# A language model's block on one core: fp16 halves transposed by DMA from SyncE instead of by TensorE

## The reference

```
h = rms_norm(rms_norm(emb[x]) @ proj.T)
h = h + attn(layernorm(h))        # 16 heads of 32; squared scores, causal, divided by their sum
                                  # ... o @ Wo.T
h = h + ffn(layernorm(h))         # fwht(x * SU_ug), gate and up (512 -> 2048), silu(gate) * up,
                                  # fwht(a * SU_dp), down (2048 -> 512)
```

## Time and profile before

| | |
|---|---|
| median of 3 runs | 1439.61 us (1438.97 to 1442.25) |
| the profiled execution | 1439.44 us, of which the span is 1437.6 us |
| granted TensorE clock, mean of the span | 0.97 of full speed |
| PE busy | 1331.6 us, 93% |

### The profile page before, as it was taken

One profiled execution on the slowest core, in us unless ns is written; L12 is line 12 of the kernel. 1 busy time (PEld: TensorE's weight loads), 2 busy tenths in 40 slices (PEclk: granted clock), 3 DMA queues, 4 the chain that ended last, 5 costly groups with the idle time before them and its releaser, 6 DMA issues.

```text
span 1437.6 us, 20304 instructions
## 1 busy us (share of the span) xinstructions
PE 1331.6 (93%) x7989; PEld 673.4 (47%) x7989; DVE 524.0 (36%) x1039; ACT 457.4 (32%) x767; POOL 418.1 (29%) x372
## 2 busy tenths in 40 slices
PE   5566439998999999999999999999999999999998
PEld 3455215554444544544444444444445445444444
DVE  1456695322522252224322442234322622251110
ACT  3475424432224312331234123322332224312220
POOL 0234212233134322442134214331343224420210
PEclk9889769999999999999999999999999999999999
DMA  9211000000100010001000010001000100010000
GB/s 332 93 61 67 22 8 1 1 1 22 38 8 1 8 45 16 1 1 47 21 0 1 30 38 1 1 23 38 8 0 9 44 16 1 1 45 15 1 1 30
DMA packets 21453, 39.41 MB, mean 27 GB/s; under 512 B 6212, under 2 KB 6520, under 8 KB 20856
## 3 DMA queue, kind: packets, MB, share of 16 engines
q1 hardware_dynamic: 17856, 28.99, 5.8%
q0 software_dynamic: 2560, 8.39, 2.0%
q10 hardware_dynamic: 952, 0.75, 0.2%
HBM read 29.47 MB, written 8.65 MB: 27 GB/s over the span
## 4 chain that ended last, share of the span: by engine, by line
PE 88%; DVE 6%; ACT 3%; issue 1%; DMA 1%; POOL 0%; SPq 0%; DVEq 0%; ACTq 0%
PE bank L1009 25%; PE bank L1010 25%; PE bank L1011 25%; PE bank L1153 3%; PE bank L1004 2%; PE bank L1138 2%; PE bank L1139 2%; ACT sg L778 2%; DMA wgu<-in_L_attn_Wv 1%; PE bank L1040 1%; PE bank L1173 1%; PE bank L1163 1%; PE bank L1002 1%; PE bank L1078 0%; DVE hid L410 0%
## 5 line engine op out<-in xcount | busy, mean ns | idle before, releaser
L1009 PE MATMUL bank<-xT,wgu 128*128 128x512 f16 x1024 | 389.1, 380 | 4.2 <-DVE xT L667 4.2
L1010 PE MATMUL bank<-xT,wgu 128*128 128x512 f16 x1024 | 389.1, 380 | 0.0
L1011 PE MATMUL bank<-xT,wgu 128*128 128x512 f16 x1024 | 389.1, 380 | 0.0
L365 POOL TENSOR_TENSOR hid<-a,hid 128x512 f16<-128x512 f32 x128 | 147.8, 1155 | 518.3 <-ACT hid L781 518.3
L701 DVE SCALAR_TENSOR_TENSOR a<-bank,kap,sg 128x512 f32<-128x512 f32 x128 | 96.1, 750 | 517.2 <-PE bank L1011 360.3
L1011 PE MATMUL bank<-wd,hid 128*128 128x512 f16 x512 | 194.8, 381 | 0.0
L1010 PE MATMUL bank<-wd,hid 128*128 128x512 f16 x512 | 194.8, 381 | 0.0
L1009 PE MATMUL bank<-wd,hid 128*128 128x512 f16 x512 | 194.8, 380 | 0.0
L337 POOL TENSOR_TENSOR p<-prod,p 128x512 f16<-128x512 f32 x128 | 149.0, 1166 | 133.8 <-ACT p L781 133.8
L781 ACT ACTIVATE hid<-a 128x512 f16<-128x512 f32 x128 | 80.6, 630 | 277.2 <-DVE a L701 277.2
L1011 PEld LDWEIGHTS bank<-xT,wgu 128*128 128x128 f16 x1024 | 100.3, 98 | 121.4 <-issue 1.1
(11 more groups left out here) (181 smaller groups left out, 1365.3 us busy)
## 6 DMA issues: line engine op xcount, KB each, us to landing
out<-a SPq DMA_DIRECT2D x24, 256.0 KB, 2.1
ids_b<-in_x SPq DMA_DIRECT2D x8, 256.0 KB, 4.0
hid<-in_L_ffn_W_gate SPq DMA_DIRECT2D x2, 1024.0 KB, 11.8
hid<-in_L_ffn_W_up SPq DMA_DIRECT2D x2, 1024.0 KB, 12.8
wd<-in_L_ffn_W_gate SPq DMA_DIRECT2D x2, 1024.0 KB, 11.7
wd<-in_L_ffn_W_up SPq DMA_DIRECT2D x2, 1024.0 KB, 10.1
hid<-in_L_ffn_W_down SPq DMA_DIRECT2D x2, 1024.0 KB, 4.8
wd<-in_L_ffn_W_down SPq DMA_DIRECT2D x2, 1024.0 KB, 4.8
```

Of the source, the lines that this page charges most:

```text
L365: nc.gpsimd.tensor_tensor(hid[:, 1, s, :], a32[:, :], hid[:, 0, s, :], ALU.subtract)\
L1009: mm(dst, w[0], v[0], start=first, stop=False)
L1010: mm(dst, w[0], v[1], start=False, stop=False)
L1011: return mm(dst, w[1], v[0], start=False, stop=final)
```

## The change

The 8 transposes on PE and the copy on ACT, for each q and each m, become one DMA transpose of the whole 128x1024 fp16 tile (256 KB), which SP issues: `o_turn(n, q)` from o16 to oT, and `x_turn(n, m)` from x16 to xn16. The slots O_FLIP_AT and X_FLIP_AT go. Waits move with them: ACT may overwrite x16 and o16 when the transfer has landed; the first gather of a block waits for the first Wo product (wo_ready) instead of the last transpose; and SP's loop over blocks is written out. SP's order while block b is fed becomes: o_turn 0 to 3, x_turn 0, store 0, x_turn 1, store 1, x_turn 2, ids_b, store 2, x_turn 3, ids_c, store 3. In the preparation the four loads of w_down and the eight turns of block 0 are mixed.

```diff
...
-O_FLIP_AT = (5, 9, 13, 17)
...
-X_FLIP_AT = (21, 23, 25, 27)
...
-        oT = sb("oT", [P, 2, QUADS, T], F16)
+        oT = sb("oT", [P, QUADS, 2, T], F16)
...
-            norm_load(2, 16)
-            norm_load(0, 20)
-            norm_load(1, 24)
...
+            def o_turn(n, q):
+                if n and q == 0:
+                    sp.wait_ge(S["wo_ready"], 4 * n)
+                sp.wait_ge(S["ol_done"], QUADS * n + q + 1)
+                nc.sync.dma_start_transpose(oT[:, q, :, :].rearrange("p l (m t) -> p (l m) t", t=P),
+                                            o16.rearrange("p l d -> p (l d)")).then_inc(S["oT_done"], 16)
+
+            def x_turn(n, m):
+                sp.wait_ge(S["xl_done"], 4 * n + m + 1)
+                if n or m:
+                    sp.wait_ge(S["xhada_ready"], 4 * n + m)
+                nc.sync.dma_start_transpose(xn16.rearrange("p (k t) -> p k t", t=P),
+                                            x16.rearrange("p l d -> p (l d)")).then_inc(S["xc_done"], 16)
+
+            def block_io(b, n, turning):
+
+                for q in range(QUADS):
+                    if turning is not None:
+                        o_turn(turning, q)
+                if turning is not None:
+                    x_turn(turning, 0)
                 for m in range(4):
                     if n is not None and m == 2:
                         load_ids_rows(n)
@@ -274,15 +287,24 @@
                         sp.wait_ge(S["y_done"], 3 * b + m + 1)
                     else:
                         sp.wait_ge(S["y_last_done"], b + 1)
-                    nc.sync.dma_start(out_rows[bass.ds(b, 1), m, :, :].rearrange("a p d -> (a p) d"), o_out[m][:, :])\
+                    nc.sync.dma_start(out_rows[b, m, :, :], o_out[m][:, :])\
                         .then_inc(S["stored"], 16)
+                    if turning is not None and m < 3:
+                        x_turn(turning, m + 1)
 
             load_ids_rows(1)
+            o_turn(0, 0)
+            norm_load(2, 16)
+            o_turn(0, 1)
+            norm_load(0, 20)
+            norm_load(1, 24)
+            o_turn(0, 2)
+            o_turn(0, 3)
+            for m in range(4):
+                x_turn(0, m)
             load_ids_columns(1)
-            with sp.Fori(0, NB - 2) as b:
-                block_io(b, b + 2)
-            block_io(NB - 2, None)
-            block_io(NB - 1, None)
+            for b in range(NB):
+                block_io(b, b + 2 if b + 2 < NB else None, b + 1 if b + 1 < NB else None)
...
-                    pool.wait_ge(S["o_flipped"], QUADS * n + QUADS)
+                    pool.wait_ge(S["wo_ready"], 4 * n + 1)
                     pool.wait_ge(S["h1_done"], 4 * n + m)
...
+                    if not (isinstance(n, int) and n == 0 and q == 0):
+                        act.wait_ge(S["oT_done"], 16 * (QUADS * n + q))
                     copy(o16[:, 0, :], wide[:, :]).then_inc(S["oh_done"], 1)
-                if s in O_FLIP_AT:
-                    q = O_FLIP_AT.index(s)
-                    act.wait_ge(S["o_flipped"], QUADS * n + q + 1)
-                    if q == 0:
-                        act.wait_ge(S["wo_ready"], 4 * n)
-                    copy(oT[:, :, q, :], banks[6][:, :].bitcast(F16).rearrange("p (l t) -> p l t", l=2))\
-                        .then_inc(S["oT_done"], 1)
-                if s in X_FLIP_AT:
-                    m = X_FLIP_AT.index(s)
-                    act.wait_ge(S["flip_ready"], 4 * n + m + 1)
-                    act.wait_ge(S["xhada_ready"], 4 * n + m)
-                    copy(xn16, PICK[0][:, :].bitcast(F16)).then_inc(S["xc_done"], 1)
                 if s in X_MIX_AT:
                     m = X_MIX_AT.index(s)
...
-                    act.wait_ge(S["flip_ready"], 4 * n + m)
+                    if not (isinstance(n, int) and n == 0 and m == 0):
+                        act.wait_ge(S["xc_done"], 16 * (4 * n + m))
                     copy(x16[:, 0, :], wide[:, :], scale=rstd[:, m:m + 1]).then_inc(S["xh_done"], 1)
...
-                    pe.wait_ge(S["oT_done"], QUADS * n + q)
+                    if not (isinstance(n, int) and n == 0 and q == 0):
+                        pe.wait_ge(S["o_done"], QUADS * n + q)
...
-                if s in O_FLIP_AT:
-                    q = O_FLIP_AT.index(s)
-                    pe.wait_ge(S["ol_done"], QUADS * n + q + 1)
-                    bank = banks[6][:, :].bitcast(F16)
-                    for l in range(2):
-                        for m in range(4):
-                            c = (4 * l + m) * P
-                            last = nc.tensor.transpose(bank[:, c:c + P], o16[:, l, m * P:(m + 1) * P], ident16)
-                    last.then_inc(S["o_flipped"], 1)
-                if s in X_FLIP_AT:
-                    m = X_FLIP_AT.index(s)
-                    pe.wait_ge(S["xl_done"], 4 * n + m + 1)
-                    pe.wait_ge(S["xc_done"], 4 * n + m)
-                    bank = PICK[0][:, :].bitcast(F16)
-                    for i in range(2):
-                        for k in range(DC):
-                            c = (DC * i + k) * P
-                            last = nc.tensor.transpose(bank[:, c:c + P], x16[:, i, k * P:(k + 1) * P], ident16)
-                    last.then_inc(S["flip_ready"], 1)
                 if s in X_MIX_AT:
                     m = X_MIX_AT.index(s)
-                    pe.wait_ge(S["xc_done"], 4 * n + m + 1)
+                    pe.wait_ge(S["xc_done"], 16 * (4 * n + m + 1))
                     pe.wait_ge(S["xT_done"], 4 * n + m)
...
-                        pe.wait_ge(S["oT_done"], QUADS * n + QUADS)
+                        pe.wait_ge(S["oT_done"], 16 * (QUADS * n + QUADS))
...
-                        last = split_mm(WOUT[m % 2][:, :], [oT[:, i, k, c] for i in range(2)],
+                        last = split_mm(WOUT[m % 2][:, :], [oT[:, k, i, c] for i in range(2)],
                                         [wo_t[:, i, k, :] for i in range(2)], k == 0, k == DC - 1)
...
```

More of the change, by code:

```diff
@@ L201, in tower @@
         onehotT_ready onehot_ready count_ready count_copied picked p_done ph_done pl_done
-        heads_ready den_done rden_done o_done oh_done ol_done o_flipped oT_done
+        heads_ready den_done rden_done o_done oh_done ol_done oT_done
         wo_ready h1_done bn_done mv_done ve_done rstd_done xs_done xa_done xm_done xh_done xl_done
-        flip_ready xc_done xhada_ready xThi_done xT_done
+        xc_done xhada_ready xThi_done xT_done
         gate_ready up_ready silu_done a_done ah_done al_done y_ready y_done y_last_done""".split()
@@ L256, in load_ids_rows @@
                 sp.wait_ge(S["onehotT_ready"], n)
-                nc.sync.dma_start(ids_b[:, :], x_rows[bass.ds(n, 1), :].broadcast_to([P, T])).then_inc(S["ids_land"], 16)
+                nc.sync.dma_start(ids_b[:, :], x_rows[n:n + 1, :].broadcast_to([P, T])).then_inc(S["ids_land"], 16)
             def load_ids_columns(n):
@@ L261, in load_ids_columns @@
                 sp.wait_ge(S["hrow_land"], 64 * n)
-                nc.sync.dma_start(ids_c[:, :], x_cols[bass.ds(n, 1), :, :].rearrange("a p c -> (a p) c"))\
-                    .then_inc(S["idc_land"], 16)
-            def block_io(b, n):
+                nc.sync.dma_start(ids_c[:, :], x_cols[n, :, :]).then_inc(S["idc_land"], 16)
+            def o_turn(n, q):
[16 more added lines that the diff above has]
+                    x_turn(turning, 0)
                 for m in range(4):
```

## The result

The changed kernel takes 1424.28 us (median of 4 runs, 1423.7 to 1428.19) against 1439.7 before; the ratio is 0.9896, 95% interval 0.9874 to 0.9917. It is 15.4 us faster, 1.1%. The forecast was 1433.6 us: the sign was right, the gain was two and a half times as large as forecast.

The account below looks back on a forecast made before the run. PE's list was taken to bound the seven blocks. Stalls of 2.5 us against 3.56 saved give -1.06 a block, x 7 = -7.4, and +1.4 in the preparation: -6.0 us, so 1433.6 us; range 1419 to 1486.

Parts of the forecast that it names:

- What is removed: On PE's list in blocks 1 to 7: 8 transpose groups of 0.4455 us each go, 3.56 us a block, 24.9 us.
- L = 3.6: Time in us of one DMA transpose from SP's issue to its semaphore, taken near the gather's 3.4; ends 2.1 and 5.4.
- 14 L: Total change given as 14 L - 56.4 us, for a transfer length L between 2.8 and 4.2 us.
- the upper bound's pieces of 32 bytes: Transfer broken into 8192 pieces of 8 ns on 16 engines: data takes 4.1 us, so a length of 5.4 us.
- oT for Wo: Transfer of o before the Wo product: 4.2 us are left, so hidden at 3.6 us; beyond that a stall.
- The ring: Single x16 and xn16 make each transfer wait for the mix before; stall L - 2.8 = 0.8 us at mix 2.
- Store 2: On SP's queue x_turn 3 is issued behind this store; stall L - 1.9 = 1.7 us at mix 3.
- The first gather: Waiting for the Wo product, it makes first h1 start 4.4 us after it instead of 0.46; preparation about +1.4 us.
- the forecast's own signs of being wrong: L outside 3 to 4.2, gathers and transfers slowing each other, SP held long by an issue, clock falling after 2 us waits.
- the clock's fall: In the slower rival, PE's long wait at mix 3 costs 2.7 us of clock, seven add 19; 1486 us, chance 0.31.
- The serial case: Rival: each transfer worked off as eight 128x128 blocks of 1.3 us, L = 10.4; about 1730 us, chance 0.11.

Follow-up runs that it names:

- The o half with the early gather: Against the kernel before: only o transposed by DMA, x still on PE; a block's first gather waits for o's last transfer; 1423.89 us.
- all three edits together: Changed kernel with first gather waiting for o's last transfer, x_turn 3 issued before store 2, and two buffers of x16 and xn16; 1411.69 us.
- The halves: Changed kernel with each DMA transpose of x split in two, the high half issued once ACT has written it; 1430.66 us.
- the runs with later transfers: Changed kernel with one or two extra unused DMA transposes of x16 ahead of each x_turn; 1446.11 and 1481.45 us.
- both with the o half: Kernel before with only o transposed by DMA: first gather waiting for the Wo product, 1434.58 us, or for o's last transfer, 1423.89 us.
- each edit alone: Changed kernel with one edit: first gather waiting for o's last transfer, 1421.98; x_turn 3 before store 2, 1422.48; two buffers of x16 and xn16, 1425.32 us.
- (a) with (b): Changed kernel with two buffers of x16 and xn16 and x_turn 3 issued before store 2, first gather unchanged; 1421.08 us.

## Why the prediction came out as it did

The mechanism was right, and the error was in sizes. Step by step:

- **What is removed, 3.56 us a block:** right. The o half with the early gather shows 1.78 us to the hundredth in three of five whole periods, and all three edits together 3.15 to 3.44 of the 3.56. The rival source of the gain, ACT's copies, does not fit: PE has no gap in the periods before or with the o half, so what shortens them is its own list.
- **L = 3.6:** mis-sized, it is 3.1 us, so -7.0 us by the forecast's own 14 L. It lay nearer the gather's 3.4 than the load's 4.0, and the upper bound's pieces of 32 bytes do not occur.
- **oT for Wo:** hidden, as forecast.
- **The ring, L - 2.8 at mix 2:** 0.30 us at L = 3.1, as measured. The halves fit the same slope: at L = 3.75 it gives 0.95, and they show 0.81 + 0.165 = 0.975.
- **Store 2, L - 1.9 at mix 3:** mis-sized; 0.65 us where it gives 1.2. The sum had 0.5 us of queueing behind the store's data, and none is seen: the transfer behind store 2 takes the usual 3.15 us to the mix. -3.9 us over seven blocks.
- **The first gather:** h1 starts 4.36 us after the Wo product (forecast 4.4). In the preparation its +1.4 us was 0: the Wo product of block 0 came earlier by nearly as much, since it no longer waited for ACT's copy (it starts at 146.70 us, against 151.23 before). What the sum missed is what the h1 chain without slack does when a gather or transfer is slow.
- **Slow gathers and transfers:** left out of the sum. Three of the seven blocks lose 0.5 to 1.1 us more than the regular one and a fourth 0.1, 2.6 us in all. One of the three, with 0.5 us, is for 0.26 us in the records (0.43 in the stream) an idle stretch with no releaser named (993.84 us), and no slow transfer.

Together: -6.0 - 7.0 - 3.9 - 1.4 = -18.3, as seven regular blocks of 2.61 us have it; + 2.6 for the irregular ones gives the -15.7 us between the two spans. The sign hung on L: the forecast crosses zero at L = 4.0, no row showed a DMA transpose, and it gave "faster" 0.46. That L lay on the gather's side and not on the load's was in part luck. That PE's list bounds the blocks and that the waits sit at mixes 2 and 3 was not.

Two of the forecast's own signs of being wrong did appear. SP is held for 1.23 us by one issue, which is part of L here and cost nothing more, until transfers were multiplied. And gathers and transfers of x were slow in some blocks, which is the 2.6 us above.

Of the rivals, the clock's fall was real in kind (the runs with later transfers) but the changed kernel stays short of it. The serial case is near what the change gives when x is transposed block by block: 1645.15 us. Each issue holds SP for 1.25 us there, and eight blocks in one instruction do not cost eight times that; they land after 3.1 us. The Trainium skill ("VectorE: DVE Perf Modes", "The three transpose paths") gives 1309 ns for one 128x128 block by DMA. The trace with eight pieces is near that figure, the one with whole tiles far below eight times it.

The marked waits at the mixes went away when gathers and transfers were issued earlier; no run had a shorter transfer at the same issue cost. The Trainium skill ("DMA: Bandwidth & Descriptors", "Rules for kernel authors") advises to issue a DMA early, compute, and wait on its semaphore late. The run with all three agrees, with 1411.69 us against 1424.28.

Open: why the second gather takes 5 us in some blocks and 3.5 in others, and the transfer 4 or more instead of 3.1. The transfers of x seem to have to do with it: the longest gather takes 3.5 us to land in the three kernels without them (before, and both with the o half), and 4.3 to 5.8 us in nine of the eleven with them. But in slow and quick blocks alike the first transfer of x is issued 2.54 us after that gather (with transfer 3 ahead of store 2: 5.34 us to h1 at 501.38, 3.48 at 1102.67), so their distance does not decide it. It was not tried to separate the two by a change of one of them alone.

## What to carry to other kernels

Where one engine is the bound, count what leaves its list by the distance of starts, then ask of each new transfer what must happen before its issue: here single buffers, an unrelated store in the same queue, and a wait put on a convenient semaphore (the Wo product instead of the transfer) took over a third of the 24.9 us, with the slow gathers and transfers. Such waits can hide each other: each edit alone, and (a) with (b), gave about 3 us or less, all three together nearly doubled the gain. Issue a DMA transpose as one large instruction, and let each wait name exactly what frees the buffer.

## What the runs showed of the hardware

- A DMA transpose on SP's queue holds SP for about 1.2 us at 256, 128 and 32 KB alike (1.23, 1.19, 1.25), up to 2.6 us now and then, where a plain transfer in the same timelines holds it for 0.33 to 0.53. Landing depends on size only in part: 3.1 us at 256 KB, 2.4 at 128 KB.
- It takes 1056 packets for 256 KB, 248 bytes each in the mean.
- Behind two waits of PE of 1.64 and 1.97 us the granted clock was 0.66 and 0.92 over the next stretches; behind 1.66 and 1.89 us in the same kernel it was 1.00, and so it was in the changed kernel, whose waits went up to 1.51 us.
- Beside DMA transposes of x some gathers took 4.3 to 5.8 us, and without them at most 3.5; the median is 3.4 in nearly every kernel. Why only some, is open.
